# A transformer block with adaptive layer norm: the setup ahead of the first batch in another order

## The reference, cut to what matters

```python
mod = silu(c) @ wmod                    # 8 x 6 x 256
sa, ca, ga, sb, cb, gb = mod            # shifts, scales and gates of both halves
g = (2 * (g >= 0) - 1) * maximum(abs(g), 0.25)          # for ga and gb
h = layernorm(x) * (1 + ca) + sa
x = x + ga * attention(h)               # 16 heads of 16; Wq, Wk, Wv, Wo and biases
h = layernorm(x) * (1 + cb) + sb
x = x + gb * (mx_quantised(h) @ mx_quantised(Wf).T + bf)
```

## Time and profile before

| | |
|---|---|
| median of 3 runs | 340.42 us (340.0 to 342.04) |
| profiled execution | 342.32 us, span 340.5 us |
| busy DVE, PE, POOL, ACT | 287.0, 270.1, 232.4, 197.5 us |
| idle DVE before batch 0's products, before step 0 | 11.69, 4.11 us |
| step 0, 1, 2 open at | 47.73, 76.06, 108.88 us |
| chain that ended last | DVE 59%, PE 20%, issue 13% |

### The profile page before, as it was taken

The page is one execution under the profiler, slowest core; times in us unless marked ns, Lnnn a source line. Parts: engine busy times, 40 slices in busy tenths (PEclk is TensorE's granted clock), DMA queues, the critical chain, the costliest instruction groups (busy, mean ns, idle before and its releaser), DMA issues.

```text
span 340.5 us, 4162 instructions
## 1 busy us (share of the span) xinstructions
PE 270.1 (79%) x1257; PEld 159.8 (47%) x1257; DVE 287.0 (84%) x337; ACT 197.5 (58%) x528; POOL 232.4 (68%) x162
## 2 busy tenths in 40 slices
PE   3789879689939895889988998899796578384756
PEld 0434346336514650574556455644553456252434
DVE  4406949989997899899999999999999999985731
ACT  2438954666785777877797777766550547220320
POOL 5101063894699979998999899989989986931210
PEclk9859969999987998999999999999999859589598
DMA  6900487495565169336945683397069511030211
GB/s 205 324 0 0 153 262 229 140 332 199 161 205 184 66 213 285 101 115 200 304 134 158 196 268 110 110 310 251 21 187 316 169 46 62 22 86 0 79 63 62
DMA packets 54386, 53.89 MB, mean 158 GB/s; under 512 B 4094, under 2 KB 52812, under 8 KB 54364
## 3 DMA queue, kind: packets, MB, share of 16 engines
q1 hardware_dynamic: 54364, 53.63, 49.8%
HBM read 44.89 MB, written 8.72 MB: 157 GB/s over the span
## 4 chain that ended last, share of the span: by engine, by line
DVE 59%; PE 20%; issue 13%; ACT 5%; DMA 1%; SPq 0%; POOL 0%; DVEq 0%; ACTq 0%
DVE prod L1238 19%; DVE pv_buf L1338 17%; PE ps L651 4%; PE ps L819 3%; DVE pv_buf L1349 3%; DVE ps L1249 2%; DVE zq L1266 2%; PE ps L663 2%; PE ps L738 2%; DVE ps L1302 2%; DVE ps L1306 2%; DVE ps L1301 2%; DVE outb L1276 2%; DVE ps L1286 1%; DMA x_in<-in_L_attn_x 1%
## 5 line engine op out<-in xcount | busy, mean ns | idle before, releaser
L524 POOL TENSOR_TENSOR pv_buf<-pv_buf 128x1024 f32<-128x1024 f32 (+2 forms) x63 | 141.9, 2252 | 30.6 <-DVE pv_buf L1338 26.8
L1238 DVE TENSOR_TENSOR prod<-ps,kT 128x1024 f32<-128x1024 f32 (+4 forms) x80 | 85.5, 1106 | 12.0 <-PE ps L663 12.0
L1338 DVE TENSOR_TENSOR pv_buf<-v_shift,ps 128x1024 f32<-128x1024 f32 x56 | 67.4, 1208 | 0.0
L738 PE MATMUL ps<-prod,sel_sum 128*32 128x512 f32 x256 | 33.2, 642 | 13.9 <-DVE prod L1238 13.9
L819 PE MATMUL ps<-wf_g,w_raw 128*128 128x256 f32 x128 | 37.5, 443 | 0.0
L651 PE MATMUL ps<-hT,wT 128*128 128x512 f32 x64 | 34.1, 684 | 1.9 <-ACT hT L966 1.9
L782 PE MATMUL ps<-wo_g,w_raw 128*128 128x256 f32 x128 | 33.4, 406 | 0.0
L506 POOL TENSOR_TENSOR rstd<-var,minus_half 128x4 f32<-128x4 f32 x8 | 8.1, 1016 | 35.2 <-ACT var L918 31.2
L819 PEld LDWEIGHTS ps<-wf_g,w_raw 128*128 128x128 f32 x128 | 26.5, 218 | 8.0 <-issue 4.3
L663 PE MATMUL ps<-hT,wT 128*128 128x512 f32 x64 | 29.3, 600 | 0.0
L680 PE MATMUL ps<-wT,h_cen 128*128 128x256 f32 x128 | 29.1, 380 | 0.0
(11 more groups left out here) (137 smaller groups left out, 518.1 us busy)
## 6 DMA issues: line engine op xcount, KB each, us to landing
v_shift<-v_rows SPq DMA_DIRECT2D x56, 512.0 KB, 5.1
x_in<-in_L_attn_x SPq DMA_DIRECT2D x8, 512.0 KB, 3.3
x_res<-in_L_attn_x SPq DMA_DIRECT2D x8, 512.0 KB, 6.8
v_rows<-v_base SPq DMA_DIRECT2D x8, 512.0 KB, 4.6
out_x<-outb SPq DMA_DIRECT2D x7, 512.0 KB, 5.2
rows_mod<-mod_rows SPq DMA_DIRECT2D x8, 256.0 KB, 3.2
pv_buf<-in_L_wmod SPq DMA_DIRECT2D x1, 1024.0 KB, 7.8
row_ga<-mod_rows SPq DMA_DIRECT2D x8, 128.0 KB, 3.9
```

The source lines that it names most:

```text
L524: nc.gpsimd.tensor_tensor(dst, dst, ring(b, n)[:, t:NT, :], ALU.add).then_inc(s_add, 1)
L738: mm = nc.tensor.matmul(ps23[32 * g:32 * g + 32, 1, :], sel_sum[:, which, c, :], prod[:, n, c, :], start=(c == 0 and which == 0), stop=(c ...
L1238: nc.vector.tensor_tensor(prod[:, n, :, o:L], ps01[:, :, o:L], kT[:, b % 2, :, 0:L - o], ALU.mult).then_inc(s_prod, 1)
L1338: nc.vector.tensor_tensor(dst[:, t:NT, :].rearrange("p t (h e) -> p t h e", e=DH), v_n.rearrange("p t (h e) -> p t h e", e=DH), weights, A ...
```

## The change

SyncE loads x of batch 0 second, ahead of the modulation columns. The FFN weight is loaded third of the weights. The rest of the modulation weight, the biases bo and bf and the residual x go out after the column parameters. The zero rows ahead of V are written at once.

TensorE opens the Q banks first. It transposes Wv and Wo before h of batch 0 and makes K and Q of batch 0 in turn by PSUM bank; K starts with one half of h. Batch 1's h is transposed into other banks, so its transposes no longer wait for V. The modulation rows are made in step 0, between Q and V of batch 1.

VectorE quantises the FFN weight in the filling and makes the products of batch 0 bank by bank, twenty of them of half the size. It also takes the statistics of batch 2's x, which were ScalarE's. The gates are formed by GpSimd in step 0, ten instructions after the power of batch 3 and before the adds 7 to 9. The split and Wo times gate of batch 0 move to the start of step 1. SyncE writes and reads the rows at the end of step 0's list.

The diff, cut to its core:

```diff
             sp.dma_start(cond_sb[:, :], cond).then_inc(s_cond, 16)
+            sp.dma_start(x_in[:, :, :], tokens(x[0])).then_inc(s_xin, 16)
+            wmod_v = wmod.rearrange("(k p) n -> p k n", p=P)
+            sp.dma_start(wmod_cols[:, :, :], wmod_v[:, :, 0:n_cols]).then_inc(s_wmod[0], 16)
...
-            n_cols = 2 * D
-            sp.dma_start(wmod_sb[:, :, 0:n_cols], wmod_v[:, :, 0:n_cols]).then_inc(s_wmod[0], 16)
-            sp.dma_start(x_in[:, :, :], tokens(x[0])).then_inc(s_xin, 16)
...
-            for i in (1, 0, 2):
+            for i in (1, 0, 4, 2, 3):
                 weight(i)
-            sp.dma_start(wmod_sb[:, :, n_cols:], wmod_v[:, :, n_cols:]).then_inc(s_wmod[1], 16)
-            weight(3)
-            weight(4)
-            sp.dma_start(brow[:, 0, :], bo.partition_broadcast(B)).then_inc(s_brow, 16)
-            sp.dma_start(brow[:, 1, :], bf.partition_broadcast(B)).then_inc(s_brow, 16)
-            sp.dma_start(x_res[:, :, :], tokens(x[0])).then_inc(s_xres, 16)
+            sp.wait_ge(s_const, CONST_ALL)
+            for i in range(2):
+                sp.dma_start(v_dram.ap()[i, 0:P], v_shift[:, 0, 0, :]).then_inc(s_vpad, 16)
+
+            def load_rest():
+                sp.dma_start(wmod_rows[:, :, :], wmod_v[:, :, n_cols:]).then_inc(s_wmod[1], 16)
+                sp.dma_start(brow[:, 0, :], bo.partition_broadcast(B)).then_inc(s_brow, 16)
+                sp.dma_start(brow[:, 1, :], bf.partition_broadcast(B)).then_inc(s_brow, 16)
+                sp.dma_start(x_res[:, :, :], tokens(x[0])).then_inc(s_xres, 16)
 
             def load_x(b):
...
+            load_x(1)
             sp.wait_ge(s_cset, SETUP_COLS)
             sp.dma_start(cols_dram.ap().rearrange("b p k -> p b k"), cols8[:, :, :]).then_inc(s_spill, 16)
-            load_x(1)
             sp.wait_ge(s_spill, 16)
             sp.dma_start(cols[:, :], cols_dram.ap()[1]).then_inc(s_cols, 16)
+            load_rest()
...
-            sp.wait_ge(s_cset, SETUP_ROWS)
-            sp.dma_start(rows_dram.ap(), rows8[:, :, :]).then_inc(s_spill, 16)
...
+
+            def spill_rows():
+                sp.wait_ge(s_rows, NROWSET)
+                sp.dma_start(rows_dram.ap(), rows8[:, :, :]).then_inc(s_spill, 16)
+                sp.wait_ge(s_spill, 32)
+                load_row_ga(0)
+                load_rows_mod(0)
+                load_row_gb(0)
+                sp.wait_ge(s_split, NGATED)
+                sp.dma_start(bias_dram.ap(), split8[:, :, :, :]).then_inc(s_spill, 16)
+                sp.wait_ge(s_spill, 48)
+                load_bias_att(0)
+                load_bias_ffn(0)
...
                 if has(b + 3):
                     load_x(b + 3)
+                if b == 1:
+                    load_row_ga(1)
...
-                load_row_ga(b + 1)
+                if b > 0:
+                    load_row_ga(b + 1)
                 shift_v(b + 1, 5)
                 shift_v(b + 1, 6)
...
                 shift_v(b + 1, 7)
+                if b == 0:
+                    spill_rows()
                 if has(b - 3):
                     store(b - 3)
...
+            def setup_rows():
+                pool.wait_ge(s_modrows, 1)
+                gates = mod_rows[:, 0::3, :]
+                nc.gpsimd.tensor_scalar(gated8[:, :, :], gates, 0.25, None, ALU.max)
+                nc.gpsimd.tensor_scalar(rest8[:, :, :], gates, -0.25, None, ALU.min)
+                nc.gpsimd.tensor_scalar(sgn[:, :, :], gates, 0.0, None, ALU.is_ge)
+                nc.gpsimd.tensor_scalar(mag[:, :, :], gates, 0.0, None, ALU.is_lt).then_inc(s_rows, 1)
+                nc.gpsimd.tensor_scalar(rows8[:, CB, :], mod_rows[:, 2, :], 1.0, None, ALU.add)
+                nc.gpsimd.tensor_copy(rows8[:, SB, :], mod_rows[:, 1, :])
+                pool.wait_ge(s_rows, 1)
+                nc.gpsimd.tensor_tensor(sgn[:, :, :], sgn[:, :, :], gated8[:, :, :], ALU.mult)
+                nc.gpsimd.tensor_tensor(mag[:, :, :], mag[:, :, :], rest8[:, :, :], ALU.mult).then_inc(s_rows, 1)
+                pool.wait_ge(s_rows, 2)
+                nc.gpsimd.tensor_tensor(rows8[:, GA:GB + 1, :], sgn[:, :, :], mag[:, :, :], ALU.add).then_inc(s_rows, 1)
+                pool.wait_ge(s_rows, 3)
+                pool.wait_ge(s_brow, 32)
+                nc.gpsimd.tensor_tensor(gated8[:, :, :], rows8[:, GA:GB + 1, :], brow[:, :, :],
+                                        ALU.mult).then_inc(s_rows, 1)
+
             def split_gated_biases():
 
-                pool.wait_ge(s_cset, SETUP_ROWS)
+                pool.wait_ge(s_rows, NROWSET)
...
-                if b == 0:
+                if b == 1:
                     split_gated_biases()
+                    gate_projection(0)
...
                     rstd_after(b - 1)
+                if b == 0:
+                    setup_rows()
...
         def _(pe):
-            pe.wait_ge(s_const, 3)
+            pe.wait_ge(s_const, 6)
+            for j in range(NC):
+                mm = nc.tensor.matmul(ps01[:, j, :], ones3[:, 0:P], ones3[:, :], start=True, stop=True)
+            mm.then_inc(s_qopen, 1)
 
...
                 pe.wait_ge(s_wmod[1], 16)
-                pe.wait_ge(s_wTe, 2)
-                modulation(ps67[0:B, 0, :], 1)
-                modulation(ps67[0:B, 1, :], 2).then_inc(s_pset, 1)
+                pe.wait_ge(s_d, 1)
+                modulation(ps67[0:B, 0, :], wmod_rows, 0)
+                modulation(ps67[0:B, 1, :], wmod_rows, 1).then_inc(s_pset, 1)
 
             weight_transposes(2)
-
-            pe.wait_ge(s_wTe, 2)
-            pe.wait_ge(s_const, 6)
-            for j in range(NC):
-                mm = nc.tensor.matmul(ps01[:, j, :], ones3[:, 0:P], ones3[:, :], start=True, stop=True)
-            mm.then_inc(s_qopen, 1)
+            weight_transposes(3)
...
+                elif b == 1:
+                    pe.wait_ge(s_wTe, 4)
                 else:
                     pe.wait_ge(s_v, NC * b - c)
+                ps = ps45 if b == 1 else ps23
...
-                for k in range(NC):
+                for k in (1, 0):
+                    pe.wait_ge(s_hT, NC * (b + 1) - k)
                     mm = nc.tensor.matmul(ps23[:, j, :], wT[:, 1, k, P * j:P * j + P], hT[:, k, :],
-                                          start=(k == 0), stop=(k == NC - 1))
+                                          start=(k == 1), stop=(k == 0))
                 mm.then_inc(s_kp, 1)
...
+                if b == -2:
+                    k_rows(0, 1)
+                    q_rows(0, 1)
+                    k_rows(0, 0)
+                    q_rows(0, 0)
+                if ahead and b >= 0:
                     k_rows(b + 2, 1)
                     k_rows(b + 2, 0)
-                if b == -1:
-                    weight_transposes(3)
                 if b == 1:
...
+            def copy_modulation_rows():
+                act.wait_ge(s_pset, 8)
+                nc.scalar.activation(mod_rows.rearrange("b m n -> b (m n)"), ps67[0:B, :, :].rearrange("b k n -> b (k n)"),
+                                     ACT.Copy).then_inc(s_modrows, 1)
...
             norm_before(0)
             evacuate_weight(1)
-            evacuate_weight(0)
             h_modulated(0, 1)
             h_modulated(0, 0)
+            evacuate_weight(0)
             evacuate_weight(2)
             evacuate_k(0, 1)
-            evacuate_k(0, 0)
             centre_h(0)
             sums_before(1)
+            evacuate_k(0, 0)
             squares_before(1)
+            evacuate_weight(3)
+            evacuate_v(0, 1)
             norm_before(1)
-            evacuate_v(0)
+            evacuate_v(0, 0)
             h_modulated(1, 1)
             h_modulated(1, 0)
...
+            def first_qk_products(c):
+                dve.wait_ge(s_q, 2 - c)
+                dve.wait_ge(s_k, 2 - c)
+                for n, o in enumerate(OFFS):
+                    ins = nc.vector.tensor_tensor(prod[:, n, c, o:L], ps01[:, c, o:L], kT[:, 0, c, 0:L - o], ALU.mult)
+                    if c == 0:
+                        ins.then_inc(s_prod, 1)
...
-            for b in STEPS:
+            setup_ffn_weight()
+            first_qk_products(1)
+            first_qk_products(0)
+            variance_before(2)
...
                     quantise(b - 2)
-                if b == -1:
-                    setup_rows()
 
```

165 lines of the change are left out of this document (71 added, 94 removed).

## The result

The kernel after takes **345.11 us** (median of 4 runs, 344.7 to 345.58) where the kernel before took 340.21 beside it: ratio 1.012, interval 1.008 to 1.016. Built and run once more it took 342.2 (10 runs, 341.08 to 345.46) against 341.15: ratio 1.005, interval 1.001 to 1.009. It is slower by half a per cent to one, where 336.6 was forecast; the first median lies above the stated range (332.0 to 341.5) and above the 343.8 to which the prediction gave a chance of 0.05. The profiled execution of after took 345.26 us around a span of 343.5.

What follows compares the result with a forecast made beforehand. Mostly VectorE's schedule bounds the kernel; the filling gains 13.0 us, of which 3.8 are kept at step 2's opening behind GpSimd's gate chain. Median 340.42 less 3.8 gives 336.6 us, range 332.0 to 341.5.

Steps and rivals of the forecast that it cites:

- What bounds the kernel: Whole kernel: mostly one long VectorE schedule, so the change is worth what it moves the first opening not held otherwise.
- The filling: Start to step 0's opening: products start at 18.2, softmax opens at 34.7 instead of 47.73, 13.0 us earlier.
- The first rival: Filling: TensorE's clock falls all the same, K and Q cost up to 6.3 us more, about 341.5; chance 0.15.
- Step 0: From step 0's to step 1's opening: slack absorbs the added work, so step 1 opens at 63.0 instead of 76.06.
- The gates: GpSimd, ahead of adds 7 to 9: ten instructions forming the gates take 7.7 us, 9.9 at the upper bound.
- the gate chain is longer: Rival, step 1: one-input work at 1.14 (+2.2), landing after 3.6 (+1.5), giving 338.8 to 340.4; chance 0.15.
- The chain behind them: Step 1, gates to step 2: split ends 79.6, bias lands and projection starts 84.5, step 2 opens 105.1, not 108.88.
- Whatever is gained and still held at the opening of step 2 goes through to the end: From step 2 to the end: the program is as before, so the 3.8 us kept there come off the total.
- The median: Whole kernel: runs of before lay 1.9 us under the profiled execution, so 338.5 profiled becomes a median of 336.6.
- VectorE's wait at the opening of step 2: End of step 1: VectorE is ready near 95 and waits about 10 us until step 2 opens near 105.
- second rival: Step 1: bias there when ScalarE is ready, step 2 opens at 98, 329.5 us; chance 0.18 together with going part way.

Runs made afterwards that it cites:

- the four at 0.60: After with its end filled and GpSimd's four gate instructions that hold a constant turned into copies: 335.61 us, against 338.43 for the filled after.
- the quantisation's run: After with the FFN weight quantised in step 1 again and three instructions added behind GpSimd's last work: 344.97 us.
- the two variants of it that open step 2 at 108.1: After with the gates formed behind adds 7 to 9: 345.58 us; after with the FFN weight quantised in step 1 again: 344.97 us.

## Why the prediction was wrong

- *What bounds the kernel* was right for the middle: from the opening of step 2 to the block maxima at 302 VectorE takes 193.7 us in both traces.
- *The filling*: right up to the products: K and Q at the upper clock (7.1 us for sixteen records), products at 18.40 for 18.2. The FFN weight took 3.1 us there (13.72 to 16.81), not 4.4, so it was hidden with room. Step 0 opened at 34.70 as forecast, but that this is the number to the tenth is luck: VectorE waited 3.10 us for the x of batch 2, whose statistics the change gave it, and the walk had no such term. The scores, which it walked to, were ready at 34.63. The first rival (a clock that falls in the filling) did not come: 1.00 from the start to 72.75.
- *Step 0*: right, 62.66 for 63.0.
- *The gates*, the term that was mis-sized: 7.7 us by four one-input instructions at the cast's 0.60; measured 12.2, by 1.49 each (3.6 us), 1.26 for 1.14 four times (0.5) and 1.24 for 0.70 in the two small ones (0.5). An instruction with a constant is not a cast, and it fell outside both bounds (0.60 and 1.14): on GpSimd it costs more than a product of two tensors, by 0.23 us. The GPSIMD Engine Reference of the Trainium skill (section 3.1) gives about 2.6 cycles per element to two-input work and 1.8 to the best case of a tight loop; this trace disagrees for instructions with a constant, which cost more than the two-input ones, and agrees for the copy, which costs less. The rival "the gate chain is longer" is what happened, past its own end of +2.2.
- *The chain behind them*: 4.0 us late at the split's end, of which 1.7 came back (spill to request 1.62 and not 2.72, landing 1.54 and not 2.1): projection at 86.77 for 84.5. From there to the opening 21.9 us for 20.6: the clock costs 3.1 in the projection (7.5 us from its first record to K's, for 4.4 before) and not 2.5, and 0.65 more at the last transposes (1.63 for 0.98), which the walk had at the upper clock. Opening 108.63 for 105.1: **3.5 us of the miss**. The errors partly cancel (4.0 late, 1.7 back, 1.3 of clock), so it is partly chance that the four's 3.6 alone equal the miss; with the four at 0.60 the opening is 104.3.
- *"Whatever is gained and still held at the opening of step 2 goes through to the end, since from there on the program is as before"* is the step that failed in kind. The program is as before, the clock is not. **3.2 us of the miss** lie behind 302, 2.8 of them behind the last residual, and filling TensorE's gaps there takes them away. The prediction had the clock's falls in the filling and in step 1 as terms and never looked at the end. There the trace of before has a fall in the middle of the last FFN: transposes at 1.10 us, then one half at 3.68 and the other at 1.99.
- The two make 6.7 us: 338.5 was forecast for the profiled execution and 345.26 measured. In after's second profile the end took as long as before's, and the opening, 108.13 for 105.1, is the whole miss (341.49 for 338.5).
- *The median* missed by 8.5 us, 1.7 more: the prediction took off the 1.9 us by which the runs of before lay under their profiled execution, while after's lay 0.15 under theirs. The trace it read was a slow one of before: step 2 opened at 106.8 to 107.8 in before's other profile and in the two with the end filled.
- *VectorE's wait at the opening of step 2*, about 10 us: 9.72, with both its ends some 4 us later than walked (98.9 for 95, 108.6 for 105), since the late adds hold VectorE too. It says that nothing done to VectorE in step 1 mattered, and the quantisation's run confirms it.
- The prediction's second rival, that the bias is there early, did not come in after, but its price was good: it had step 2 at 98, and with the gates left out or on VectorE and the filling whole it opened at 98.0 to 98.5.

Not settled: why after falls into the upper group more often than before (15 of 25 runs at 344.7 or more in after and the two variants of it that open step 2 at 108.1; none of before over 343.2), although before's end has the same gaps of 4.8 and 2.55 us. No run here separates what decides where the clock falls.

## What to carry to other kernels

A gain in the filling counts only as far as the last of the chains behind it: walk each (here gates, adds, split, spill, landing, projection) instruction by instruction, and price each by its own kind of instruction; with no such row in the trace, the range has to reach past the dearest neighbour. Where TensorE's matmuls alternate with gaps, as in this kernel's end, the same work cost 3 us more or less by where the granted clock fell, so two kernels that differ early are compared fairly only with that part held still. Filling the gaps with unread matmuls (3.6 us off after's 342.2, 2.5 to 3.6 off before) gained more than the change itself, which gained nothing as it stood. Small setup work is cheap only where no chain waits for it: the same gates, moved to VectorE, brought after from its 342 to 345 us down to 334.3. Small work moved to an engine next to a busy one may be the victim: look at its durations in place.

## What was not expected of the hardware

- GpSimd over 8x512 float32: 1.48 to 1.49 us with a constant, 0.60 a copy, 1.03 to 1.26 with two tensors.
- VectorE's instructions with a constant over 8x512 took 2.31 and 2.02 us beside GpSimd's adds of 128x1024 and 0.41 without them; the one with two inputs 1.65 and 0.68. The adds took the same either way (5.72 and 5.71 for three). The Trainium skill (SBUF — State Buffer, "Who interferes with whom") says that the two engines share a port pair as an exclusive lock, which the second to issue waits for; these rows agree: 2.31 is about the 1.91 of one add and 0.41. It goes the other way too: GpSimd's power took 1.93 and not 1.02 us right behind the start of a VectorE product of two SBUF tensors.
- The end of the kernel takes 27.2 us at a clock that fifteen added matmuls hold at 1.00, and 30.4 or 33.2 without them, for the same wanted instructions.
